# A one-column clear on GpSimd, and a wait for its signal, between the gathers of a graph-network kernel

## Chip, cores and metric

The kernel runs on 1 core of one Trainium2 chip. The metric is device time in microseconds (us) of one execution. The kernel before takes 1381.97 us, the median of three runs (1381.46 to 1383.72).

## What is computed

The reference works on 6250 nodes with 256 features and 100,000 edges. Two layers follow one another, each added to its input:

```python
# layer 1: layer norm, sum over edges, two linear layers
h = _layernorm(x)
h = segment_sum(h[dst], src, 6250) + h
x = x + ((h @ gW1 + gb1) @ gW2 + gb2)
# layer 2: layer norm, router over 8 experts, each with three 256x256 products
y = _layernorm(x)
w = softmax(mean(y[None], axis=0) @ Wr + br)
h = relu(bn1(y @ W1[e] + b1[e]));  h = relu(bn2(h @ W2[e] + b2[e]))
x = x + sum_e w[:, e] * (h @ Wo[e] + bo[e])
```

## The kernel before

Nodes stand in 49 bins of 128 rows. The linear layers of layer 1 are multiplied into one 256x256 matrix, which is applied to the nodes first; the projected rows are stored in HBM as two float16 halves (`xn_hilo`, 512 columns a row). The edges are sorted by bin on the chip in a first phase that fills some 235 us of the profile, and cut into 830 entries (`NENT`) of 128 edges each, 415 pairs.

An entry is worked as follows. GpSimd issues one indirect DMA (a gather, L544) that brings 128 rows of `xn_hilo`, one for each edge of the entry, into a slot of `gbuf`. VectorE builds a 128x128 matrix of ones and zeros (`onehot`, L1002), TensorE multiplies the two (L1504 and L1505, two matmuls an entry, four a pair), and VectorE adds the result to the bin's rows in `acc` (L1071).

`gbuf` has 18 slots (`SLOTS`), so nine pairs (`RING`). Entry k uses slot k % 18. From k = 18 on, an even k waits until TensorE has counted up the semaphore `ent_done` for the pair that had the slot before, nine pairs ago. TensorE waits for each gather's own semaphore (`gathered0` to `gathered17`) before it reads the slot.

Layer 2 runs in 15 groups of 1, 2, 3 or 4 bins (`GS`), 8 experts each, which makes 120 steps. In each step TensorE does the first product of the next expert (`L1`, L1555, into PA), the second of this one (`L2`, L1571, into PB) and the third of the one before (`L3`, L1589). ScalarE and VectorE turn the products into float16 halves (L730, L741, L1167, L1173), and VectorE weighs the third product into the output (L1190). Layer 1 and layer 2 overlap: a plan spreads pairs over the steps, three to five a step, so that the bins of group g + 1 are complete when layer 2 reaches them. The first 13 pairs are worked before the first step; the last 11 steps have no pairs. Each engine's instructions stand in the order in which the code issues them.

GpSimd does small set-up work in the first 41 us of the profile, then waits for the sorted edges, and from there on does nothing but issue gathers. The array `idle` has two columns; column 0 is cleared by VectorE at L1110 and neither column is read by anything.

Of the kernel before, what the change touches and what calls it, by code (L numbers as in the profile page):

```python
# [58 lines left out]
SLOTS = 18  # L59
# [84 lines left out]
def build(nc, x, src, dst, gW1, gb1, gW2, gb2, Wr, br, bn, W1, W2, Wo, bo, out):  # L144
    xn_dram = nc.dram_tensor("xn_hilo", (NPAD, 2 * D), F16, kind="Internal").ap()
    x_dram = nc.dram_tensor("x_whole_bins", (NPAD, D), F32, kind="Internal").ap()
    with ExitStack() as ctx:
        def sb(name, shape, dt):
            return ctx.enter_context(nc.sbuf_tensor(name, shape, dt))
# [4 lines left out]
        def sem(name):  # L154
            return ctx.enter_context(nc.semaphore(name))
# [10 lines left out]
        idle = sb("idle", [P, 2], F32)  # L166
# [125 lines left out]
            "xt_in0", "xt_in1", "xb_ready", "x2_ready", "sd_ready", "y_ready",  # L292
            "yT_done", "yhi_ready", "ylo_ready", "lg_done", "ex_ready", "w_ready", "wT_done", "wT_sb",
            "bo_done", "bo_added", "l1_done", "l2_done", "l3_done", "z1_ready", "z2_ready", "lo1_ready", "lo2_ready",
            "y3_added", "out0", "out1", "ord_ready", "mem0")}
        wst_in = [sem(f"wst_in{i}") for i in range(16)]
        gat = [sem(f"gathered{i}") for i in range(SLOTS)]

# [97 lines left out]
        def _(sp):  # L396
# [25 lines left out]
            def load_weights(pieces):  # L422
                for n in pieces:
                    w, width, _, _ = piece(n)
                    old = ahead(n)
                    if 8 <= place(n) < 12:
                        sp.wait_ge(s["turned"], 4 * 6 + 2)
                    elif place(n) >= 4 and old is None:
                        sp.wait_ge(s["sched_pe"], 6 + NBLK)
                    if old is not None:  # L430
                        sp.wait_ge(s["whi_ready"], old + 1)
                        if by_pe(old):
                            sp.wait_ge(s["wlo_ready"], place_by_pe(old))
                        else:
                            sp.wait_ge(s["wlo_dve"], place_by_dve(old))
                    sp.dma_start(stage(n)[:, :, 0:width], w).then_inc(wst_in[place(n)], 16)
# [16 lines left out]
            def load_x(g):  # L453

                _, b = nc.values_load_multi_w_load_instructions(
                    ordi[0:1, FIRST[g]:FIRST[g + 1]], engines=[ENG.SP], min_val=0, max_val=BINS - 1,
                    skip_runtime_bounds_check_because=IN_RANGE)
                for i in range(GS[g]):
                    sp.dma_start(xt[:, g % 2, i, :], x_dram[bass.ds(b[i] * P, P), :]).then_inc(s[f"xt_in{g % 2}"], 16)

            def store(g):

                _, b = nc.values_load_multi_w_load_instructions(
                    ordi[0:1, FIRST[g]:FIRST[g + 1]], engines=[ENG.SP], min_val=0, max_val=BINS - 1,
                    skip_runtime_bounds_check_because=IN_RANGE)
                sp.wait_ge(s["y3_added"], all_thirds(EX * g + EX - 1))
                for i in range(GS[g]):
                    sp.dma_start(out[bass.ds(b[i] * P, P), :], xt[:, g % 2, i, :]).then_inc(s[f"out{g % 2}"], 16)
# [13 lines left out]
        @block.gpsimd  # L482
        def _(pool):
            c = [0]

            def step(ins):
                c[0] += 1
                ins.then_inc(s["consts"], 1)

            pool.memset(acc[:, BINS - 1, :], 0.0).then_inc(s["mem0"], 1)  # L490
            step(pool.memset(ident[:], 0.0))
            step(pool.iota(pidx[:], pattern=[[0, 1]], base=0, channel_multiplier=1))
            step(pool.iota(iri[:], pattern=[[1, P]], base=0, channel_multiplier=0))
            step(pool.iota(pcoli[:], pattern=[[1, NBLK]], base=0, channel_multiplier=NBLK))
            step(pool.memset(ones[:], 1.0))
            step(pool.memset(epsln[:], EPS_LN))
            step(pool.memset(epsbn[:], EPS_BN))
            step(pool.memset(cnt[:], 0.0))
            step(pool.iota(cbi, pattern=[[P, BINS + 1]], base=0, channel_multiplier=0))
            step(pool.iota(iotk.bitcast(I32), pattern=[[1, NENT]], base=0, channel_multiplier=0))  # L500
            pool.wait_ge(s["consts"], 10)
            step(pool.affine_select(out=ident[:], in_=ident[:], compare_op=ALU.not_equal, fill=1.0, base=0,
                                    pattern=[[-1, P]], channel_multiplier=1))
            step(pool.tensor_copy(iota_row[:], iri[:]))
            step(pool.tensor_copy(pcol[:], pcoli[:]))
            step(pool.tensor_copy(bcol[:], pidx[:]))
            step(pool.tensor_copy(tk, iotk.bitcast(I32)))
            step(pool.tensor_copy(cbf, cbi))
            pool.wait_ge(s["consts"], 16)
            step(pool.tensor_copy(iotk, tk))  # L510
            step(pool.tensor_scalar(nid[:], ident[:], -1.0, None, ALU.mult))
            step(pool.tensor_scalar(wid[:], ident[:], WS, None, ALU.mult))

            step(pool.tensor_scalar(cntb[:], cbf, -1.0, 0.5, ALU.mult, ALU.add))
            step(pool.memset(negd[:], -1.0 / D))
            step(pool.tensor_scalar(cmat[:], ident[:], -1.0 / D, None, ALU.add))

            split = [0]

            def bias(ins):  # L520
                split[0] += 1
                ins.then_inc(s["bo_split"], 1)
                pool.wait_ge(s["bo_split"], split[0])

            high, low = nst[0:3 * EX, 2, 0:D], bolow[:]
            pool.wait_ge(s["small_in"], 16 * 16)
            bias(pool.tensor_scalar(lowrow[:, 1:2], bcol[0:3 * EX, :], 2 * EX - 0.5, None, ALU.is_gt))
            bias(pool.tensor_scalar(lowrow[:, 0:1], lowrow[:, 1:2], -1.0, 1.0, ALU.mult, ALU.add))
            bias(pool.tensor_copy(high, bosb[:]))
            bias(pool.tensor_tensor(low, bosb[:], high, ALU.subtract))  # L530
            bias(pool.tensor_scalar(low, low, lowrow[:, 1:2], None, ALU.mult))
            bias(pool.tensor_scalar(bosb[:], high, lowrow[:, 0:1], None, ALU.mult))
            bias(pool.tensor_tensor(bo3[:], bosb[:], low, ALU.add))

            for i in range(4):
                pool.wait_ge(s[f"nst_stored{i}"], 16 * ((TWOS - 1 - i) // 4 + 1))
            pool.wait_ge(s["first_ready"], 1)

            for k in range(NENT):
                if k == TK_SLOT or k == SLOTS:  # L540
                    pool.wait_ge(s["ord_ready"], 1)
                if k >= SLOTS and k % 2 == 0:
                    pool.wait_ge(s["ent_done"], k // 2 - RING + 1)
                pool.indirect_dma_start(gbuf[:, k % SLOTS, :], None, xn_dram,  # L544
                                        bass.IndirectOffsetOnAxis(dsti[:, k:k + 1], 0)).then_inc(gat[k % SLOTS], 16)

# [1161 lines left out]
```

## Time and profile before

| | |
|---|---|
| median of 3 runs | 1381.97 us |
| span of the profiled execution | 1595.0 us |
| TensorE matmul, busy in the span | 1279.8 us (80%) |
| VectorE, busy | 1197.4 us (75%) |
| ScalarE, busy | 868.3 us (54%) |
| GpSimd, busy | 805.0 us (50%) |
| 16 DMA engines, gathers' queue | 23.8% of the span |
| mean granted TensorE clock | 0.928 |

Busy shares are of the profiled span, which is 213 us longer than the median of the runs that are timed without a profile. What surrounds the span isn't listed for the profiled execution, so its own time is known by the span alone. In the rows below, a bracket [x <-y] behind an instruction is the time that its engine sat idle ahead of it, and what released it.

### The profile page before, as it was taken

The page shows a single profiled execution, that of the slowest core. Times are in us where ns is not written, and L with a number is a line of the kernel's source. Part 1 is how long each engine was busy: PE and PEld are TensorE (multiplying, and loading weights), DVE is VectorE, ACT ScalarE, POOL GpSimd, SP SyncE. Part 2 cuts the span into 40 slices and gives each one's busy share as a digit, 9 for nine tenths or more (in the row PEclk, how much of TensorE's full clock was granted, in tenths as well). Part 3 has the DMA queues.
Part 4 walks back from the last instruction along what each step waited for, and adds up shares of the span by engine and source line. Part 5 has one row for each costly group of instructions (what it writes and reads, how often), then busy time and mean ns, then how long its engine had stood idle before and what let it go on. Part 6 is the DMA issues. An engine that isn't in the chain of part 4 may idle for free.

```text
span 1595.0 us, 25908 instructions
## 1 busy us (share of the span) xinstructions
PE 1279.8 (80%) x8179; PEld 841.9 (53%) x8179; DVE 1197.4 (75%) x3476; ACT 868.3 (54%) x1623; POOL 805.0 (50%) x864
## 2 busy tenths in 40 slices
PE   3868885557687778888878878898888998788998
PEld 3746652345454445455545545554555666565665
DVE  9999985566667666777777877777778887777865
ACT  7887451344455435454445544555545665555685
POOL 3000006666556666666666666666666556656300
PEclk9969997778799988999999999999999999999999
DMA  9301135333232332333333333343333323332200
GB/s 292 99 0 53 54 100 170 109 98 103 83 103 86 110 91 87 111 88 100 102 89 113 87 90 113 87 116 87 89 111 88 107 83 107 88 105 86 74 11 11
DMA packets 82235, 150.86 MB, mean 95 GB/s; under 512 B 16855, under 2 KB 55034, under 8 KB 82100
## 3 DMA queue, kind: packets, MB, share of 16 engines
q0 software_dynamic: 39840, 108.84, 23.8%
q1 hardware_dynamic: 42260, 40.36, 8.0%
q8 instruction: 67, 1.10, 0.3%
q14 instruction: 68, 0.56, 0.1%
HBM read 129.87 MB, written 19.27 MB: 94 GB/s over the span
## 4 chain that ended last, share of the span: by engine, by line
PE 47%; DVE 24%; issue 12%; another core or an unknown queue 8%; ACT 7%; DVEq 2%; ACTq 0%
PE PA L1555 11%; PE PB L1571 11%; DVE acc L1071 5%; PE PL L1589 4%; DVE zz L837 4%; PE PT L1589 4%; PE PN L1589 3%; DVE zz L838 3%; DVE onehot L1002 2%; DVE xt L1190 2%; ACT PB L742 2%; PE PN L1505 2%; PE PT L1505 1%; PE PT L1504 1%
## 5 line engine op out<-in xcount | busy, mean ns | idle before, releaser
L544 POOL DMA_INDIRECT gbuf<-xn_hilo,dsti x830 | 790.3, 952 | 667.5 <-issue 196.8
L741 ACT ACTIVATE h<-PB,bnt,bns 128x512 f16<-128x512 f32 (+3 forms) x240 | 167.7, 699 | 325.9 <-remote 177.5
L1555 PE MATMUL PA<-yT,wsplit 128*128 128x512 f16 (+3 forms) x1440 | 318.1, 361 | 13.0 <-issue 9.4
L1571 PE MATMUL PB<-h,wsplit 128*128 128x512 f16 (+3 forms) x1440 | 300.3, 347 | 5.6 <-issue 5.6
L730 ACT ACTIVATE h<-PA,bnt,bns 128x512 f16<-128x512 f32 (+3 forms) x240 | 167.8, 699 | 215.8 <-remote 104.2
L1555 PEld LDWEIGHTS PA<-yT,wsplit 128*128 128x128 f16 x1440 | 143.3, 103 | 114.9 <-issue 31.3
L1173 DVE TENSOR_TENSOR h<-PB,h 128x512 f16<-128x512 f32 (+3 forms) x240 | 139.9, 587 | 84.8 <-ACT PB L742 64.5
L1571 PEld LDWEIGHTS PB<-h,wsplit 128*128 128x128 f16 x1440 | 141.2, 101 | 98.3 <-issue 13.0
L1002 DVE TENSOR_SCALAR onehot<-iota_row,srel 128x128 f16<-128x128 f16 x830 | 178.2, 267 | 0.0
L1167 DVE TENSOR_TENSOR h<-PA,h 128x512 f16<-128x512 f32 (+3 forms) x240 | 139.5, 587 | 40.2 <-ACT PA L731 31.8
L1071 DVE TENSOR_TENSOR acc<-acc,PN 128x256 f32 x276 | 114.0, 413 | 71.9 <-issue 23.8
L731 ACT ACTIVATE PA<-PA,bnt,bns 128x512 f32<-128x512 f32 (+3 forms) x240 | 160.8, 670 | 0.0
L742 ACT ACTIVATE PB<-PB,bnt,bns 128x512 f32<-128x512 f32 (+3 forms) x240 | 160.6, 669 | 0.0
L1071 DVE TENSOR_TENSOR acc<-acc,PT 128x256 f32 x286 | 118.0, 413 | 46.5 <-remote 16.1
L1071 DVE TENSOR_TENSOR acc<-acc,PL 128x256 f32 x268 | 110.6, 413 | 51.6 <-remote 21.1
L1589 PE MATMUL PN<-wsplit,h 128*128 128x256 f16 x792 | 104.9, 281 | 24.2 <-DVE xt L1190 7.2
L1589 PE MATMUL PL<-wsplit,h 128*128 128x256 f16 x828 | 107.6, 278 | 18.9 <-DVE acc L1071 6.3
L1589 PE MATMUL PT<-wsplit,h 128*128 128x256 f16 x732 | 96.1, 280 | 14.9 <-DVE acc L1071 7.2
L1589 PEld LDWEIGHTS PN<-wsplit,h 128*128 128x128 f16 x792 | 77.6, 100 | 50.1 <-issue 32.5
L1589 PEld LDWEIGHTS PL<-wsplit,h 128*128 128x128 f16 x828 | 80.1, 99 | 45.1 <-issue 24.7
L1504 PE MATMUL PN<-gbuf,onehot 128*128 128x256 f16 x276 | 72.2, 286 | 36.8 <-issue 28.8
L1504 PE MATMUL PL<-gbuf,onehot 128*128 128x256 f16 x268 | 70.7, 287 | 35.5 <-issue 30.6
(250 smaller groups left out, 1856.5 us busy)
## 6 DMA issues: line engine op xcount, KB each, us to landing
gbuf<-xn_hilo,dsti POOLq DMA_INDIRECT x830
xt<-x_whole_bins SPq DMA_DIRECT2D x49, 128.0 KB
out<-xt SPq DMA_DIRECT2D x49, 128.0 KB
acc<-in_x SPq DMA_DIRECT2D x4, 1536.0 KB
x_whole_bins<-acc SPq DMA_DIRECT2D x4, 1536.0 KB, 11.8
xn_hilo<-xt SPq DMA_DIRECT2D x24, 256.0 KB, 2.1
h<-in_L_ffn_W SPq DMA_DIRECT2D x9, 256.0 KB, 4.3
zz<-in_L_ffn_W SPq DMA_DIRECT2D x5, 256.0 KB
```

What stands on the lines that cost most here:

```text
L544: pool.indirect_dma_start(gbuf[:, k % SLOTS, :], None, xn_dram, bass.IndirectOffsetOnAxis(dsti[:, k:k + 1], 0)).then_inc(gat[k % SLOTS], 16)
L730: nc.scalar.activation(h1[:, e % 2, 0, h, 0:w], PA[:, h, 0:w], ACT.Relu, bias=sh, scale=sc)
L731: nc.scalar.activation(PA[:, h, 0:w], PA[:, h, 0:w], ACT.Relu, bias=sh, scale=sc).then_inc(s["z1_ready"], 1)
L741: nc.scalar.activation(h2[:, e % 2, 0, h, 0:w], PB[:, h, 0:w], ACT.Relu, bias=sh, scale=sc)
L742: nc.scalar.activation(PB[:, h, 0:w], PB[:, h, 0:w], ACT.Relu, bias=sh, scale=sc).then_inc(s["z2_ready"], 1)
L1002: ins = V.tensor_scalar(onehot[:, k % SLOTS, :], iota_row[:], srel[:, k:k + 1], None, ALU.is_equal)
L1071: V.tensor_tensor(to, to, bank(("E", p))[:, i, :], ALU.add).then_inc(s["acc_done"], 1)
L1173: V.tensor_tensor(h2[:, e % 2, 1, h, 0:w], PB[:, h, 0:w], h2[:, e % 2, 0, h, 0:w], ALU.subtract).then_inc(s["lo2_ready"], 1)
L1504: T_.matmul(to[:, i, :], onehot[:, m, :], gbuf[:, m, 0:D], start=True, stop=False)
L1555: last = T_.matmul(PA[:, h, 0:w], wsp[0][:, e, k, wp, h * P:(h + 1) * P], yT[:, g % 2, yp, k, 0:w], start=n == 0, stop=n == 5)
L1571: last = T_.matmul(PB[:, h, 0:w], wsp[1][:, e, k, wp, h * P:(h + 1) * P], h1[:, e % 2, yp, k, 0:w], start=n == 0, stop=n == 5)
L1589: last = T_.matmul(to[:, i % 2, :], h2[:, e % 2, yp, k, i * P:(i + 1) * P], wsp[2][:, e, k, wp, :], start=n == 0, stop=n == 5)
```

## The change

From the 20th gather on (k = 19), GpSimd clears column 1 of `idle` (128 partitions, one float32 each) ahead of every gather, 811 times in all, and the gather waits for the semaphore `paced`, which that clear counts up. The wait for a free slot, where there is one, stands ahead of the clear.

```diff
-            "y3_added", "out0", "out1", "ord_ready", "mem0")}
+            "y3_added", "paced", "out0", "out1", "ord_ready", "mem0")}
...
                 if k >= SLOTS and k % 2 == 0:
                     pool.wait_ge(s["ent_done"], k // 2 - RING + 1)
+                if k > SLOTS:
+                    pool.memset(idle[:, 1:2], 0.0).then_inc(s["paced"], 1)
+                    pool.wait_ge(s["paced"], k - SLOTS)
                 pool.indirect_dma_start(gbuf[:, k % SLOTS, :], None, xn_dram,
                                         bass.IndirectOffsetOnAxis(dsti[:, k:k + 1], 0)).then_inc(gat[k % SLOTS], 16)
```

The instructions of GpSimd before, from the 19th gather on, with the semaphores that each waits for:

```order
L544 DMA gbuf<-xn_hilo,dsti 128x512 [waits ent_done,ord_ready]
L544 DMA gbuf<-xn_hilo,dsti 128x512
L544 DMA gbuf<-xn_hilo,dsti 128x512 [waits ent_done]
L544 DMA gbuf<-xn_hilo,dsti 128x512
L544 DMA gbuf<-xn_hilo,dsti 128x512 [waits ent_done]
```

The same place of GpSimd's stream in the changed kernel:

```order
L547 DMA gbuf<-xn_hilo,dsti 128x512 [waits ent_done,ord_ready]
L545 MEMSET idle 128x1
L547 DMA gbuf<-xn_hilo,dsti 128x512 [waits paced]
L545 MEMSET idle 128x1 [waits ent_done]
L547 DMA gbuf<-xn_hilo,dsti 128x512 [waits paced]
L545 MEMSET idle 128x1
L547 DMA gbuf<-xn_hilo,dsti 128x512 [waits paced]
L545 MEMSET idle 128x1 [waits ent_done]
L547 DMA gbuf<-xn_hilo,dsti 128x512 [waits paced]
```

A clear stands between any two gathers, the wait for a slot has moved from the gather to the clear, and each gather waits for the clear just ahead of it. The other engines keep their instructions in the same order.

## Rows read from the trace of the kernel before

**Rows 1.** The page: busy time, share of the span and instructions of each engine.

```profile
PE 1279.8 (80%) x8179; PEld 841.9 (53%) x8179; DVE 1197.4 (75%) x3476; ACT 868.3 (54%) x1623; POOL 805.0 (50%) x864
```

**Rows 2.** The waits of GpSimd: us in total, times, longest.

```profile
POOL gbuf L544 <- issue: 196.8, 641, 0.7
POOL gbuf L544 <- DVE dsti L1012: 195.7, 1, 195.7
POOL gbuf L544 <- remote: 125.2, 75, 4.2
POOL gbuf L544 <- PE PN L1505: 51.1, 37, 2.8
POOL gbuf L544 <- PE PL L1505: 50.4, 38, 2.5
POOL gbuf L544 <- PE PT L1505: 48.3, 38, 2.2
```

**Rows 3.** The gathers by source line: duration in ns, min/median/max.

```profile
L544 POOL DMA_INDIRECT gbuf<-xn_hilo,dsti x830: 941/947/1952, 235.8 to 1497.0; - x166
```

**Rows 4.** Timeline of GpSimd, 905 to 911 us: start us, us.

```profile
905.74 0.95 POOL L544 DMA_INDIRECT gbuf<-xn_hilo,dsti  x1 [0.30 <-issue]
906.99 0.95 POOL L544 DMA_INDIRECT gbuf<-xn_hilo,dsti  x1 [0.30 <-issue]
909.67 0.94 POOL L544 DMA_INDIRECT gbuf<-xn_hilo,dsti  x1 [1.73 <-PE PN L1505]
910.92 0.94 POOL L544 DMA_INDIRECT gbuf<-xn_hilo,dsti  x1 [0.30 <-issue]
```

**Rows 5.** Timeline, 857 to 862 us: pair 198 on TensorE, gather into its slot.

```profile
857.64 0.27 PE L1505 MATMUL PN<-gbuf,onehot 128*128 128x256 f16 x1
...
861.59 0.94 POOL L544 DMA_INDIRECT gbuf<-xn_hilo,dsti  x1 [1.89 <-remote]
```

**Rows 6.** Timeline, 1190 to 1192 us: pair 307 on TensorE, gather into its slot.

```profile
1190.75 0.27 PE L1505 MATMUL PT<-gbuf,onehot 128*128 128x256 f16 x1
...
1191.29 0.94 POOL L544 DMA_INDIRECT gbuf<-xn_hilo,dsti  x1 [2.25 <-PE PT L1505]
```

**Rows 7.** Timeline: gathers 2, 8, 27 and 28, and pair 3 (of gathers 7 and 8) on TensorE.

```profile
237.32 1.27 POOL L544 DMA_INDIRECT gbuf<-xn_hilo,dsti  x1 [0.30 <-issue]
245.60 0.95 POOL L544 DMA_INDIRECT gbuf<-xn_hilo,dsti  x1 [0.30 <-issue]
...
249.66 0.27 PE L1504 MATMUL PN<-gbuf,onehot 128*128 128x256 f16 x1
...
268.16 0.94 POOL L544 DMA_INDIRECT gbuf<-xn_hilo,dsti  x1 [0.31 <-issue]
273.26 0.95 POOL L544 DMA_INDIRECT gbuf<-xn_hilo,dsti  x1 [4.15 <-remote]
```

**Rows 8.** Timeline: the last gather's start, and TensorE's last matmul of an entry.

```profile
1496.96 0.94 POOL L544 DMA_INDIRECT gbuf<-xn_hilo,dsti  x1 [0.31 <-issue]
...
1516.73 0.27 PE L1505 MATMUL PT<-gbuf,onehot 128*128 128x256 f16 x1
```

**Rows 9.** Timeline of GpSimd: one-column clears; instructions waiting for the one ahead.

```profile
1.73 0.09 POOL L496 MEMSET epsln<- 128x1 f32 x1
1.76 0.09 POOL L497 MEMSET epsbn<- 128x1 f32 x1
...
33.60 0.41 POOL L528 TENSOR_SCALAR lowrow<-lowrow 24x1 f32<-24x1 f32 x1
34.08 0.80 POOL L529 CAST onehot<-bosb 24x256 f16<-24x256 f32 x1
```

**Rows 10.** VectorE's onehot matrices by source line: duration in ns, min/median/max.

```profile
L1002 DVE TENSOR_SCALAR onehot<-iota_row,srel x830: 241/247/496, 237.7 to 1497.3; 128x128 f16<-128x128 f16 x166
```

**Rows 11.** VectorE, L1190, in 1350 to 1490 us, then in 1505 to 1590 us.

```profile
L1190 DVE SCALAR_TENSOR_TENSOR xt<-PN,w,xt x18: 472/475/485, 1357.0 to 1484.2; 128x256 f32<-128x256 f32 x18
...
L1190 DVE SCALAR_TENSOR_TENSOR xt<-PN,w,xt x14: 472/475/483, 1507.7 to 1588.6; 128x256 f32<-128x256 f32 x14
```

## The prediction

> **What bounds the kernel now.** The page's busy times come first [rows 1]: TensorE 1279.8 us and VectorE 1197.4 us of a span of 1595.0 us, GpSimd only 805.0 us. By these GpSimd looks half idle. But nearly all its work is 830 gathers in a row, so I ask how much of its idle time between them is real slack.
>
> The list of its waits [rows 2] splits that time. 195.7 us is the one wait for the sorted edges, ahead of the first gather. 196.8 us in 641 pieces is "issue": 0.30 us each, with nothing waited for. The other four rows (125.2, 51.1, 50.4 and 48.3 us, together 275.0 us in 188 pieces; "remote" is a release that the view can't place) are waits for a free slot of `gbuf`. A gather takes 0.947 us [rows 3] and follows the one before 0.30 us after its end even where nothing holds it up: the starts 905.74 and 906.99 us lie 1.25 us apart [rows 4]. So 1.25 us is the shortest spacing of two gathers before. The 188 slot waits hold 0.30 us of it each (56 us), which leaves 219 us of real slack in the profiled execution, 0.26 us a gather.
>
> The timed runs have less. The span is 1595.0 us, the median of the runs 1382.0 us, so 213 us of the profiled execution isn't in them. Rows show one place where it may lie: TensorE starts the last matmul of a pair at 857.64 us (0.27 us long), and the gather that needs its slot starts only at 861.59 us, after 1.89 us of idle GpSimd, 3.7 us after that matmul's end [rows 5]; at another pair the same distance is 1190.75 + 0.27 to 1191.29, 0.27 us [rows 6]. TensorE's signals come late by microseconds in the profile, and everybody waits for them. I read this as a cost of the profiling (an inference). What it takes off the timed runs comes off GpSimd's slack: if all 213 us lie in the phase of the gathers, 219 - 213 = 6 us of slack are left; if they lie evenly over the span, 1262/1595 of them, 168 us, do (the gathers start from 235.8 to 1497.0 us [rows 3]), and 51 us are left. The middle is 28 us, 0.035 us a gather.
>
> A chain over GpSimd alone says the same: 235.8 us to the first gather, 830 x 1.25 = 1038 us of gathers, 4 us from the start of the last one to its use (gather 8 starts at 245.60 us and its pair is at 249.66 us on TensorE [rows 7]), and 78.3 us from the last entry's matmul (1516.73 us [rows 8]) to the end of the span: 1356 us. About 5 us more is lost at the start of the phase, where a gather sits idle 4.15 us instead of 0.31 us for its slot [rows 7]. So GpSimd alone asks for 1361 of 1382 us. **In the timed runs the gathers are within some 20 us of being the bound**, though in the profile they aren't.
>
> **What the change adds.** Nothing is removed. 811 times a one-column clear and a wait stand between two gathers. Before, the time from the end of one gather to the start of the next was 0.30 us. Now it is a sum of three:
>
> - From the gather's end to the clear's start. No row shows another instruction behind a gather. Lower bound: 0, as clears follow each other back to back (1.73 and 1.76 us [rows 9]). Upper bound: the 0.30 us after which a gather follows a gather [rows 4]. Between them I take 0.06 us, the distance at which a small dependent instruction follows the one ahead (33.60 + 0.41 to 34.08 us, 0.07 [rows 9]).
> - The clear itself: 0.09 us [rows 9].
> - From the clear's end to the gather's start, by way of a semaphore. Nearest row: a gather released by TensorE starts 0.27 us after the matmul's end [rows 6]. A small dependent instruction does it in 0.07 us [rows 9], but it isn't a gather, and gathers have 0.30 us even without a wait, so I take 0.27 us.
>
> Sum 0.42 us in place of 0.30 us: +0.12 us, a spacing of 1.37 us. With the bounds of the first term it is +0.06 us (1.31) or +0.36 us (1.61).
>
> What is queued behind the added wait: the next gather and all later ones, nothing else, since GpSimd has no other work by then; TensorE waits for those gathers, VectorE and ScalarE for TensorE. The clear writes a column that nobody reads, so no other engine waits for it. It moves behind the slot wait as well, so where a slot is late, the gather now starts 0.09 + 0.27 + the signal's way later than it would have; that is the same 0.1 us or so again, inside the sum above.
>
> **The sum.** 811 x 0.12 = 97 us more on GpSimd. In the profiled execution the slack of 219 us would cover it: I expect its span to stay near 1595 us (the lateness of TensorE's signals sets it), up to 30 us above. The timed runs have 28 us of cover, so they pay 97 - 28 = 69 us: **1451 us**. The chain over GpSimd gives nearly the same: 235.8 + 19 x 1.25 + 811 x 1.37 + 4 + 78.3 + 5 = 1458 us. I say 1452 us, +5.1%. Within this case the clear's distance behind a gather (0.03 to 0.10 us) and the slack (51 to 6 us) give 1382 + 811 x 0.09 - 51 = 1404 to 1382 + 811 x 0.16 - 6 = 1506 us, where both ends at once are unlikely: 1415 to 1485 us.
>
> One thing may come on top. VectorE builds 830 onehots of 0.247 us [rows 10], 205 us or 16% of the phase of the gathers. If GpSimd can't write while one of them runs, a clear waits in 16% of the cases for half of it: 811 x 0.16 x 0.12 = 16 us. In favour: the second gather took 1.27 us, in the stretch where VectorE builds the first onehots [rows 7]. Against: the median of all gathers, which also run beside onehots, is 947 ns with a minimum of 941 [rows 3]. I leave it out. By the Trainium skill, page SBUF — State Buffer, section Who interferes with whom, a VectorE instruction that uses both ports locks GpSimd out of the shared pair until it ends, and whoever starts first keeps it; by that rule the sum would be 1468 us. The gathers' median doesn't bear that out for this phase, so the rule moves the range's upper half and not the forecast.
>
> **The rivals.**
>
> The clear costs as a gather does (the upper bound): +0.36 us a gather, 292 us on GpSimd, 1382 + 292 - 28 = 1646 us. It would be so if the 0.30 us belonged to the gather ahead, as its tail, and not to the gather behind. Against it: a gather that waited for TensorE needs 0.27 us from the signal with no gather just ahead of it [rows 6], so most of the 0.30 us is the starting of a gather.
>
> The cost is hidden: the profiler also stretches the gathers, and in the timed runs they follow each other faster than 1.25 us, so slack is larger than 28 us. It decides at a slack of 97 us, which needs a spacing before of 1.25 - 69/811 = 1.165 us. The time is then 1382 us, with no change beyond 2.8 us. For it: GpSimd is 50% busy [rows 1] and a profile of instructions isn't free. Against: the constant 0.947 us. Between this and the forecast lies a partial case, slack 64 to 94 us: 1385 to 1415 us.
>
> Faster: spaced gathers disturb VectorE less. If the onehots, 241 ns at least and 496 at most [rows 10], cost their 6 ns between median and minimum less and now and then more, 830 x 0.02 = 17 us come back, and the time is 1365 us, provided GpSimd isn't the bound. Against: L1190 takes 475 ns with gathers beside it and 475 without any [rows 11], and the change takes no gather away.
>
> **How the numbers follow.** Forecast 0.54 (1415 to 1485 us, at its edges to 1404 and 1506); the partial case 0.15 (1385 to 1415); hidden, no change 0.14 (1380 to 1385); the dear clear 0.09 (1500 to 1646); faster 0.05 (1365 to 1379); anything else 0.03, slower. The range 1381 to 1490 us leaves out the dear clear, the faster case and the edges. A measurement of this kernel tells about 0.2% from no change, 2.8 us. Slower by more: 0.54 + 0.15 + 0.09 + 0.03 = 0.81. Within it 0.14. Faster 0.05.
>
> **What the changed profile would show.** A MEMSET of 0.09 us between gathers, starting some 0.06 us after one's end; the next gather 0.27 us after its end; spacing 1.37 us where no slot is waited for. The waits for slots shrink from 275 us to some 180 or less, and the span moves by at most 30 us, far less than the timed runs. TensorE begins to wait for gathers ahead of L1504, if slack ran out in the profile too. The forecast is wrong if the spacing is under 1.29 us (the time then moves by less than some 5 us), if it is over 1.5 us, or if the spacing is as forecast and the timed runs don't move: then the slack in them was larger than the profile lets one infer, because the lateness that I put down to profiling isn't what takes 213 us away, or because gathers run faster without it.

## The result, and the profile after

The changed kernel takes 1442.0 us (four runs, 1440.5 to 1442.4), the kernel before in the same job 1382.7 us (four runs). The ratio is 1.043, with a 95% interval of 1.0415 to 1.0444: 59 us slower. The profiled execution has a span of 1440.6 us. The prediction said 1452 us for the time and a span near 1595 us. The first was close; the second was not, and that turned out to be the more instructive part.

The page of the changed kernel, with the line that answers to [rows 1], and its chain of work that ended last:

```profile
span 1440.6 us, 26719 instructions
...
PE 1229.0 (85%) x8179; PEld 815.0 (57%) x8179; DVE 1196.9 (83%) x3476; ACT 878.3 (61%) x1623; POOL 901.5 (63%) x1675
...
POOL 58%; issue 16%; DVE 14%; PE 9%; DMA 2%; ACT 1%; DVEq 0%; ACTq 0%; POOLq 0%
POOL gbuf L547 51%; POOL idle L545 7%; DVE zz L840 5%; DVE zz L841 5%; PE PB L1574 2%; DMA gbuf<-xn_hilo,dsti 2%; PE PA L1558 2%; PE PT L1592 1%; PE PN L1592 1%; PE PL L1592 1%; PE PA L1415 1%; DVE zz L850 0%; PE PT L1372 0%; DVE zz L925 0%; DVE zz L852 0%
```

GpSimd is busy only 63% of the span, yet gathers and clears are 58% of the chain that ends last, and TensorE 9%. "Busy" leaves out the time in which a gather is being started, and 803 starts of 0.27 us (217.3 us in the next view) are nearly all of the 16% of "issue".

GpSimd's waits, which answer to [rows 2]:

```profile
POOL gbuf L547 <- POOL idle L545: 217.3, 803, 0.3
POOL gbuf L547 <- DVE dsti L1015: 194.1, 1, 194.1
...
POOL gbuf L547 <- issue: 18.5, 26, 1.6
```

The 275 us of slot waits are gone. GpSimd waits for nothing but its own clears (217.3 / 803 = 0.27 us each). TensorE waits for gathers instead:

```profile
PE PL L1507 <- DMA gbuf<-xn_hilo,dsti: 40.5, 53, 2.3
PE PT L1507 <- DMA gbuf<-xn_hilo,dsti: 36.2, 55, 3.1
PE PN L1507 <- DMA gbuf<-xn_hilo,dsti: 35.9, 54, 1.4
```

The timeline of GpSimd, which answers to [rows 4] and gives the three terms of the sum (start us, us):

```profile
904.57 0.94 POOL L547 DMA_INDIRECT gbuf<-xn_hilo,dsti  x1 [0.27 <-POOL idle L545]
905.51 0.11 POOL L545 MEMSET idle<- 128x1 f32 x1
905.90 0.94 POOL L547 DMA_INDIRECT gbuf<-xn_hilo,dsti  x1 [0.27 <-POOL idle L545]
906.84 0.11 POOL L545 MEMSET idle<- 128x1 f32 x1
908.59 0.94 POOL L547 DMA_INDIRECT gbuf<-xn_hilo,dsti  x1 [1.63 <-issue]
```

Gather's end to clear 0.00 us, clear 0.11, start of the next gather 0.27: the gathers start 905.90 - 904.57 = 1.33 us apart, where [rows 4] has 1.25. The last row is an extra stall of 1.36 us (1.63 us idle where 0.27 is usual) with nothing waited for; it comes eight times, every 130 us.

The clears and gathers by source line (duration in ns, min/median/max, first and last start), the second answering to [rows 3]:

```profile
L545 POOL MEMSET idle<- x811: 112/113/223, 259.1 to 1356.3; 128x1 f32 x163
...
L547 POOL DMA_INDIRECT gbuf<-xn_hilo,dsti x830: 944/944/2084, 234.2 to 1356.6; - x166
```

The end of the phase, which answers to [rows 8]:

```profile
1356.65 0.94 POOL L547 DMA_INDIRECT gbuf<-xn_hilo,dsti  x1 [0.27 <-POOL idle L545]
...
1360.68 0.27 PE L1508 MATMUL PT<-gbuf,onehot 128*128 128x256 f16 x1
```

TensorE uses the last gather 4.0 us after its start, about 1.3 us after its data have landed (2.7 us in the median); in [rows 8] it was 19.8 us. From there to the end it takes 79.9 us, against 78.3.

### The profile page after: what moved, and what is told of

It reads as the page before. It is cut to its first block, busy times and chain, and to the rows that moved or that the text cites. A ratio compares the mean times of both kernels' runs of the same rounds, so it can differ in the third digit from the quotient of the medians.

```text
span 1440.6 us, 26719 instructions
## 1 busy us (share of the span) xinstructions
PE 1229.0 (85%) x8179; PEld 815.0 (57%) x8179; DVE 1196.9 (83%) x3476; ACT 878.3 (61%) x1623; POOL 901.5 (63%) x1675
## 4 chain that ended last, share of the span: by engine, by line
POOL 58%; issue 16%; DVE 14%; PE 9%; DMA 2%; ACT 1%; DVEq 0%; ACTq 0%; POOLq 0%
POOL gbuf L547 51%; POOL idle L545 7%; DVE zz L840 5%; DVE zz L841 5%; PE PB L1574 2%; DMA gbuf<-xn_hilo,dsti 2%; PE PA L1558 2%; PE PT L1592 1%; PE PN L1592 1%; PE PL L1592 1%; PE PA L1415 1%; DVE zz L850 0%; PE PT L1372 0%; DVE zz L925 0%; DVE zz L852 0%
## 5 line engine op out<-in xcount | busy, mean ns | idle before, releaser
L547 POOL DMA_INDIRECT gbuf<-xn_hilo,dsti x830 | 792.0, 954 | 429.9 <-POOL idle L545 217.3
L1558 PE MATMUL PA<-yT,wsplit 128*128 128x512 f16 (+3 forms) x1440 | 299.1, 347 | 4.1 <-DVE wsplit L1201 2.6
L1574 PE MATMUL PB<-h,wsplit 128*128 128x512 f16 (+3 forms) x1440 | 294.6, 343 | 0.0
L1558 PEld LDWEIGHTS PA<-yT,wsplit 128*128 128x128 f16 x1440 | 139.2, 100 | 94.7 <-issue 5.7
L1507 PE MATMUL PT<-gbuf,onehot 128*128 128x256 f16 x286 | 75.8, 280 | 39.2 <-DMA gbuf<-xn_hilo,dsti 36.2
L1592 PE MATMUL PL<-wsplit,h 128*128 128x256 f16 x828 | 103.3, 273 | 1.6 <-ACT PB L745 1.4
L1592 PE MATMUL PN<-wsplit,h 128*128 128x256 f16 x792 | 100.6, 276 | 4.4 <-issue 3.9
L545 POOL MEMSET idle<- 128x1 f32 x811 | 94.8, 117 | 0.7
L1592 PE MATMUL PT<-wsplit,h 128*128 128x256 f16 x732 | 92.0, 274 | 1.9 <-ACT PB L745 1.4
```

The costliest lines, as they stand in the source:

```text
L545: pool.memset(idle[:, 1:2], 0.0).then_inc(s["paced"], 1)
L1507: T_.matmul(to[:, i, :], onehot[:, m, :], gbuf[:, m, 0:D], start=True, stop=False)
L1558: last = T_.matmul(PA[:, h, 0:w], wsp[0][:, e, k, wp, h * P:(h + 1) * P], yT[:, g % 2, yp, k, 0:w], start=n == 0, stop=n == 5)
L1574: last = T_.matmul(PB[:, h, 0:w], wsp[1][:, e, k, wp, h * P:(h + 1) * P], h1[:, e % 2, yp, k, 0:w], start=n == 0, stop=n == 5)
L1592: last = T_.matmul(to[:, i % 2, :], h2[:, e % 2, yp, k, i * P:(i + 1) * P], wsp[2][:, e, k, wp, :], start=n == 0, stop=n == 5)
```

## The experiments

### The kernel before, profiled again

No edit. What was expected:

> The kernel before, unchanged, profiled a second time. Theory A (the profiler holds up TensorE's signals in this kernel, by chance or always): the median of the timed runs stays near 1382 us. If it is always so, the span is again near 1595 us; if it was chance, the span is near 1381 us, the gathers lie 1.25 us apart with hardly any wait for a slot, and TensorE waits for gathers. Theory B (the long span shows how the kernel really runs): the span is 1595 us and so is the time.

Measured: 1381.2 us (one run), span **1379.4 us**, not 1595. Page, GpSimd's waits, and its timeline over the stretch of [rows 4]:

```profile
span 1379.4 us, 25908 instructions
...
PE 1210.4 (88%) x8179; PEld 817.7 (59%) x8179; DVE 1191.7 (86%) x3476; ACT 876.9 (64%) x1623; POOL 809.3 (59%) x864
...
PE 42%; POOL 21%; DVE 16%; issue 9%; DMA 8%; ACT 3%; DVEq 0%; ACTq 0%; POOLq 0%
```

```profile
POOL gbuf L544 <- issue: 227.9, 748, 0.3
...
POOL gbuf L544 <- PE PL L1505: 10.7, 33, 0.7
POOL gbuf L544 <- PE PN L1505: 8.1, 26, 0.4
POOL gbuf L544 <- PE PT L1505: 7.4, 22, 0.8
```

```profile
905.18 0.95 POOL L544 DMA_INDIRECT gbuf<-xn_hilo,dsti  x1 [0.30 <-issue]
906.43 0.97 POOL L544 DMA_INDIRECT gbuf<-xn_hilo,dsti  x1 [0.30 <-issue]
907.70 0.95 POOL L544 DMA_INDIRECT gbuf<-xn_hilo,dsti  x1 [0.30 <-issue]
```

The slot waits are 26.2 us in 81 pieces, 0.30 us of each being the start of a gather: 2 us of slack, not 219. The first profile showed an execution in which TensorE's signals came late; in this one, and in the eight other profiles of this study, they don't. So it was that one execution, not profiling as such. What made it so isn't known.

The chain above gives TensorE 42% and GpSimd 21%. It follows whatever was released last, and between two waits for a gather that is TensorE's own work, so it doesn't by itself say who sets the pace; the light kernel below does.

This second profile is the right one to set beside the changed kernel. Two more of its rows, the last gather and the last entry on TensorE:

```profile
1282.11 0.95 POOL L544 DMA_INDIRECT gbuf<-xn_hilo,dsti  x1 [0.30 <-issue]
...
1301.11 0.27 PE L1505 MATMUL PT<-gbuf,onehot 128*128 128x256 f16 x1
```

At the end of the phase TensorE runs 19.0 us behind the gathers. It wasn't so all along. TensorE's waits for gathers, 300 to 1060 us:

```profile
PE PL L1504 <- DMA gbuf<-xn_hilo,dsti: 21.5, 29, 1.8
PE PN L1504 <- DMA gbuf<-xn_hilo,dsti: 18.3, 29, 1.6
PE PT L1504 <- DMA gbuf<-xn_hilo,dsti: 16.0, 23, 1.9
```

These are 55.8 of the 64.0 us that TensorE waits for gathers in all. Up to some 1050 us GpSimd's spacing sets the time. Then comes the last group of four bins. The pairs worked beside it are those of a group of three, so a step has three pairs where it had four or five, but TensorE's layer-2 work is still that of four bins. Two steps begin like this:

```profile
1060.78 1.46 PE L1555 MATMUL PA<-yT,wsplit 128*128 128x512 f16 x6
...
1069.89 1.46 PE L1555 MATMUL PA<-yT,wsplit 128*128 128x512 f16 x6
```

A step takes TensorE 9.1 us here, and its six gathers take 7.5 us, so TensorE is the slower one. A gather that starts at 1023.50 us is used after 5.3 us, one that starts at 1114.37 us after 21.4 us:

```profile
1135.75 0.27 PE L1505 MATMUL PT<-gbuf,onehot 128*128 128x256 f16 x1
```

From 1127 us on, in the groups of three bins, the distance stays between 18 and 22 us and is 19.0 at the end. In the changed kernel it is 13.2 us at the same entry, and its slower gathers let TensorE catch up to 4.0 us by the end. **The 15 us between 19.0 and 4.0 are the cover of the kernel before.**

### The clear without the wait

```diff
                 if k > SLOTS:
+                    if k > SLOTS + 1:
+                        pool.wait_ge(s["paced"], k - SLOTS - 1)
                     pool.memset(idle[:, 1:2], 0.0).then_inc(s["paced"], 1)
-                    pool.wait_ge(s["paced"], k - SLOTS)
```

> The clear stays between any two gathers, but no gather waits for it (each clear waits for the clear before the last gather, long done). Theory A (three steps in series: clear 0.11 us, then 0.27 us to start the gather): without the wait the gather's start-up runs beside the clear, the spacing falls from 1.328 us to 1.25 to 1.29 us, and the time to 1382 to 1412 us. Rival (what costs is the clear's place in GpSimd's queue or its write, not the wait): spacing 1.33 us and 1442 us as in the changed kernel.

Measured: 1389.1 us, ratio to the kernel before 1.0049 (1.0034 to 1.0063). Its timeline:

```profile
805.29 0.95 POOL L548 DMA_INDIRECT gbuf<-xn_hilo,dsti  x1 [0.19 <-POOL idle L547]
806.23 0.12 POOL L547 MEMSET idle<- 128x1 f32 x1
806.54 0.95 POOL L548 DMA_INDIRECT gbuf<-xn_hilo,dsti  x1 [0.19 <-issue]
```

The clear stands in the 0.30 us that pass between two gathers anyway, and the spacing is again 1.25 us. The wait makes the cost: it puts the clear (0.11) and the start of a gather (0.27) in series. What is left, 7 us, goes with eight stalls of about 0.9 us that come every 121 us here, as the 1.36 us ones do in the changed kernel; that they cause all of it wasn't tested.

### Two clears

```diff
                 if k > SLOTS:
-                    pool.memset(idle[:, 1:2], 0.0).then_inc(s["paced"], 1)
-                    pool.wait_ge(s["paced"], k - SLOTS)
+                    for turn in range(2):
+                        pool.memset(idle[:, 1:2], 0.0).then_inc(s["paced"], 1)
+                        pool.wait_ge(s["paced"], 2 * (k - SLOTS) - 1 + turn)
```

> Two clears ahead of each gather, each waited for. Theory A (time follows GpSimd's spacing, 811 times): the second clear adds 0.11 us and 0.07 to 0.09 us for a small instruction that waits for the one ahead, so spacing 1.51 to 1.53 us and 1442 + 811 x 0.19 = 1596 us (1585 to 1610). Rival (the loss of the changed kernel is a one-off of the slot waits or of contention, not a price for each gather): under 1500 us.

Measured: 1571.9 us, ratio 1.1367 (1.1343 to 1.1391), which is 130 us above the changed kernel, not 154. Its timeline (the two clears are merged into one row):

```profile
805.79 0.94 POOL L548 DMA_INDIRECT gbuf<-xn_hilo,dsti  x1 [0.27 <-POOL idle L546]
806.74 0.27 POOL L546 MEMSET idle<- 128x1 f32 x2
807.28 0.94 POOL L548 DMA_INDIRECT gbuf<-xn_hilo,dsti  x1 [0.27 <-POOL idle L546]
```

The spacing is 1.49 us, 0.16 us above the changed kernel, and 811 x 0.16 = 130 us. I had put the second clear with its wait 0.03 us too high (0.19 us). With no cover left, each added nanosecond between gathers costs 811 ns.

### Every second gather

```diff
-                if k > SLOTS:
+                if k > SLOTS and k % 2:
                     pool.memset(idle[:, 1:2], 0.0).then_inc(s["paced"], 1)
-                    pool.wait_ge(s["paced"], k - SLOTS)
+                    pool.wait_ge(s["paced"], (k - SLOTS + 1) // 2)
```

> The clear and the wait only ahead of odd entries, 406 in place of 811. Theory A with no cover left in the kernel before: half of the loss, 1382.7 + 30 = 1412 us. With the cover of 28 us that was predicted for the timed runs, and a spacing that rose by 0.075 us, it would be 1382.7 + 30 - 28 = 1385 us. The two differ by 27 us, so this run measures the cover.

Measured: 1412.3 us, ratio 1.0213 (1.019 to 1.0235), 31 us for 406 clears. A cover of 28 us is ruled out. Its last gather and last entry:

```profile
1323.63 0.94 POOL L547 DMA_INDIRECT gbuf<-xn_hilo,dsti  x1 [0.27 <-POOL idle L545]
...
1332.58 0.27 PE L1508 MATMUL PT<-gbuf,onehot 128*128 128x256 f16 x1
```

That half the clears cost half of the 59 us is in part chance, since only one of the terms goes with their number. The last gather starts 41.5 us later than in the kernel before: 406 x 0.078 = 32 us of spacing and, as in the changed kernel, eight stalls of 1.36 us, 11 us. TensorE's distance behind it shrinks from 19.0 to 9.0 us, so 10 us are covered, and 31 us are left.

### A third less TensorE work in layer 2

```diff
-PASSES = [(0, 0), (0, 1), (1, 0)]
+PASSES = [(0, 0), (0, 1)]
```

and the last pass of a product stops the accumulation at 3 in place of 5 (the router's product loses the same pass). Once on the kernel before, once on the changed one.

> The kernel before with two of the three float16 passes in each product of layer 2 (the third, with the weights' low half, is left out), so a third less TensorE work in L1, L2 and L3; the result is less exact. Theory A (GpSimd's gathers already bound the kernel before): only the last 80 us, which have no gathers, shrink, by a quarter or so: 1360 us (1350 to 1370), and gathers stay 1.25 us apart. Rival (TensorE bounds it, GpSimd has cover): 936 us of matmuls in layer 2 fall by a third, the time to 1100 to 1200 us or to GpSimd's limit if that is lower.

> The changed kernel with the same third of TensorE's work in layer 2 left out. Theory A: 60 us above the light kernel before, as with the full work: 1420 us. Rival (the clear's cost comes from its meeting with TensorE's and VectorE's work): the difference changes with that work, under 40 us or over 80.

Measured: 1359.5 us (ratio to the kernel before 0.984, 0.9823 to 0.9857) and 1431.9 us (1.0363, 1.0346 to 1.038). TensorE's busy time falls from 1210.4 to 1028.6 us in the kernel before and the time by only 22 us. The last gather and the last entry of the light kernel before:

```profile
1280.66 0.95 POOL L544 DMA_INDIRECT gbuf<-xn_hilo,dsti  x1 [0.30 <-issue]
...
1284.55 0.27 PE L1505 MATMUL PT<-gbuf,onehot 128*128 128x256 f16 x1
```

The last gather starts at 1280.7 us, 1.4 us earlier than with the full work: the gathers come no faster for it, and TensorE waits for them 164.6 us instead of 64.0. That shows directly that GpSimd paced the kernel before. TensorE is now 3.9 us behind at the end instead of 19.0, so the 15 us of cover are gone, and the clears cost more here: 72 us, not the 60 that I expected.

The 1360 us forecast for the light kernel before was met by luck. I expected the stretch behind the gathers to give the 20 us; it gave 5.6 us (78.3 to 72.7). The other 15 us are that same distance, which I hadn't seen yet.

### Half the rows in every odd gather

```diff
+                rows = 64 if k > SLOTS and k % 2 else P
-                pool.indirect_dma_start(gbuf[:, k % SLOTS, :], None, xn_dram,
-                                        bass.IndirectOffsetOnAxis(dsti[:, k:k + 1], 0)).then_inc(gat[k % SLOTS], 16)
+                pool.indirect_dma_start(gbuf[0:rows, k % SLOTS, :], None, xn_dram,
+                                        bass.IndirectOffsetOnAxis(dsti[0:rows, k:k + 1], 0)).then_inc(gat[k % SLOTS], 16)
```

> The kernel before, with 64 rows in place of 128 in every odd gather from entry 19 on (the other 64 rows of those slots keep older data, so half of the edges of every second entry are wrong). How long GpSimd takes for 64 rows no run shows; between 0.5 and 0.947 us. Theory A (gathers are the bound): with any real saving the time falls at once, until TensorE and VectorE bind: TensorE stood idle for gathers some 64 us in the kernel before, so 1320 to 1370 us. Rival (not the bound): 1382 us.

> The changed kernel with the same 64-row odd gathers (same rows left out). Theory A: if the saving of the half gathers is more than the clears' 61 us, the clears are covered here, and the loss against the half-row kernel without clears is under 60 us, down to 0 where GpSimd waits for slots again; if the saving is small it is 60 us. Rival (the clears cost 60 us whatever GpSimd's slack is): 60 us above it.

Measured: 1371.9 us (ratio 0.9926, 0.9909 to 0.9942) and 1430.7 us (1.0355, 1.0337 to 1.0372). The timeline of the first:

```profile
803.68 0.90 POOL L545 DMA_INDIRECT gbuf<-xn_hilo,dsti  x1 [0.30 <-issue]
804.89 0.96 POOL L545 DMA_INDIRECT gbuf<-xn_hilo,dsti  x1 [0.30 <-issue]
806.15 0.90 POOL L545 DMA_INDIRECT gbuf<-xn_hilo,dsti  x1 [0.30 <-issue]
```

64 rows take 0.90 us, 128 take 0.96: nearly the whole gather is a fixed cost. The saving is small, so GpSimd stays the bound, and the clears cost 59 us as before. This pair therefore doesn't tell the theory from its rival ("60 us whatever GpSimd's slack is"). It shows only that a saving on GpSimd reaches the time. The half gathers have a median of 0.904 us where the kernel before has 0.946, but the full ones between them rise to 0.959, so 405 x (0.042 - 0.013) = 12 us come off GpSimd, and 9 us arrive. GpSimd's waits for slots don't grow for it (21.0 us against 26.2). Why the full gathers take longer wasn't tested.

## Why the prediction was right, and where it was not

**The direction and its reason** held: GpSimd's gathers were the bound of the timed runs although GpSimd looked half idle. The argument that found it was the chain over GpSimd, 1361 of 1382 us; by the second profile it is 1282.1 + 4 + 78.3 = 1364 us, and the 15 us left to the span of 1379.4 are TensorE's distance. The light kernel and the two clears show it from both sides.

**The spacing.** I had +0.12 us; measured +0.08 us (1.33 against 1.25). The three terms: gather's end to clear 0.06 forecast, 0.00 measured; clear 0.09 forecast, 0.11 measured; clear to gather 0.27 forecast and measured. The failed step is the first. I took the distance of small dependent instructions, but the clear depends on nothing that is late, and the row of clears that follow back to back [rows 9] was the nearer one. (Those two start 0.03 us apart and take 0.09 us each, so they overlap; and the pair that I took 0.06 us from stands 0.07 us apart. Neither slip moves the forecast by more than 8 us.)

**What the spacing missed.** From the last gather of the second profile of before to that of the changed kernel it is 1356.65 - 1282.11 = 74.5 us. 811 x 0.078 = 63 us of it is the spacing (medians of 1.329 and 1.251 us), and 8 x 1.36 = 11 us are the stalls of the kind that the timeline above shows at 907 us, which I hadn't foreseen. They come at regular distances, counted in gathers. The gathers from one stall to the next, both ends counted in, with 811, 1622 and 406 clears:

```profile
L547 POOL DMA_INDIRECT gbuf<-xn_hilo,dsti x97: 944/944/1106, 519.1 to 648.9; - x97
...
L548 POOL DMA_INDIRECT gbuf<-xn_hilo,dsti x97: 944/944/1403, 550.3 to 696.0; - x97
...
L547 POOL DMA_INDIRECT gbuf<-xn_hilo,dsti x97: 942/945/1297, 511.2 to 637.7; - x97
```

Every 96th gather stalls in each of them, eight times in all, however many clears there are. In the changed kernel with half the rows in odd gathers it is every 111th, and the three kernels without clears that were profiled after the result have none. What the stalls are wasn't tested.

**The cover.** I had 28 us (6 to 51); measured 15 us. That it lies in the range is luck, because the term was another thing: I took GpSimd's waits for slots, of which 2 us are real, while what covers is the shrinking of TensorE's distance behind the last gather from 19.0 to 4.0 us. 74.5 - 15.0 + 1.6 us (the tail, 79.9 against 78.3) = 61.1 us, and the spans differ by 61.2. The sum by its measured terms is then 63 + 11 - 15 + 2 = 61 us where I had 97 - 28 = 69: the cost 23 us too large (97 against 63 + 11) and the cover 13 us too large, errors that partly cancel.

**The span.** "I expect its span to stay near 1595 us" was wrong by 154 us. The step behind it, that profiling delays TensorE's signals in this kernel, was an inference from one execution, and the second profile refutes it. The timed runs were right all along, and a profiled execution that is 15% off the median of the timed runs should have been treated as an odd one. What saved the forecast was that the sum was made for the timed runs.

**The rivals.** The dear clear (+0.36 us) fell: the 0.30 us between gathers is the start of the second. The hidden cost fell: the profiler doesn't stretch the gathers. The second profiled execution of before took 1381.2 us and that of the changed kernel 1442.4, in line with all the runs (medians 1382.7 and 1442.0), and the gathers of the former lie 1.25 us apart. The faster case fell: VectorE's onehots have a median of 250 ns in the changed kernel against 247. The meeting with VectorE that I left out of the sum is small: the clear takes 113 ns in the median and up to 223 ns; 42 of the 811 are over 150 ns, and all that is over 113 ns sums to 3.3 us, not 16. The longest one, beside VectorE's rows:

```profile
866.61 0.41 DVE L1005 TENSOR_SCALAR onehot<-iota_row,srel 128x128 f16<-128x128 f16 x2
866.82 0.22 POOL L545 MEMSET idle<- 128x1 f32 x1
```

It begins in the first of two onehots and ends at 867.04 us, just behind the second. Of the 42 long clears 39 begin while a onehot runs and end 23 to 32 ns behind one's end, and all 39 begin with 120 ns or more of it to go. But 172 clears begin while a onehot runs, and the other 133 aren't held up; 92 of those begin with less than 120 ns of it to go. My 16 us let every meeting wait. By the Trainium skill, page SBUF — State Buffer, section Who interferes with whom, a VectorE instruction that uses both ports keeps GpSimd out until it ends. The ends of the long clears agree with that, but it isn't a price for every meeting, and no run here took VectorE's work away to test it.

## What to carry to other kernels

Judge a queue of like instructions by its spacing times its count plus what lies ahead of it and behind it, not by its busy share: here 50 to 60% busy was the bound. A small instruction fits into the 0.30 us in which GpSimd starts the next gather anyway, and there 811 clears cost 7 us. A wait for it puts it ahead of that start, in series, and then the same clears cost 59 us. And when the profiled span is far from the timed runs, take a second profile before reading slack out of the first.

## What the runs showed of the hardware that I had not expected

A gather of 128 rows of 1 KB keeps GpSimd 0.95 us and one of 64 rows 0.90 us, with 0.30 us between gathers in either case. The Trainium skill, page DMA: Bandwidth & Descriptors, section Anatomy of one DMA — SWDGE (gpsimd) path, says that many descriptors can be emitted before their cost shows, which these rows bear out. The same section gives about 50 ns for a dispatch; here a gather starts 0.27 us after the signal that it waits for, and that is the number that decided this change.

One execution of the kernel before had a span of 1595 us in the profiler with TensorE's signals microseconds late, another 1379 us with none late. And with clears between the gathers, GpSimd stalls for 1.36 us at every 96th gather, 11 us in all, as much with 406 clears as with 1622.
